# Two chained cross-attention layers: pairing the second layer's value sums, moving one set of transposes, and splitting a small softmax between VectorE and ScalarE

## The reference

```python
# layer 0: 8 heads of 40, 371 keys; the last 4 context rows are "tokens"
hs = mha(x @ Wq, enc @ Wk, enc @ Wv)
ca_q1 = einsum('btc,th->bch', ca, Wq_ca)[:, indices, :]    # 112 rows
ca_hs1 = mha(ca_q1, x, x)                                  # 112 x 112 softmax, 8 heads
ca_hs2 = mha(ca_hs1 @ Wq, ca @ Wk_ca, ca @ Wv_ca)          # 4 keys
x = (hs + ca_hs2) @ Wout + b_out + x
# layer 1: 20 heads of 16, 375 keys
x = mha(x @ Wq1, ctx @ Wk1, ctx @ Wv1) @ Wo + bo + x
```

## Time and profile before

| | |
|---|---|
| median of 3 runs | 744.45 us (744.38 to 744.81) |
| the profiled execution | 745.43 us |
| its span, first to last instruction | 743.6 us |
| mean granted TensorE clock | 0.981 |
| PE busy | 702.2 us, 94% |
| PE weight loads busy | 612.6 us, 82% |
| DVE busy | 470.8 us, 63% |
| ACT busy | 403.7 us, 54% |
| POOL busy | 294.8 us, 40% |

### The profile page before, as it was taken

One profiled execution on the slowest core, in us unless ns is written; L12 is line 12 of the kernel. 1 busy time (PEld: TensorE's weight loads), 2 busy tenths in 40 slices (PEclk: granted clock), 3 DMA queues, 4 the chain that ended last, 5 costly groups with the idle time before them and its releaser, 6 DMA issues.

```text
span 743.6 us, 18194 instructions
## 1 busy us (share of the span) xinstructions
PE 702.2 (94%) x6924; PEld 612.6 (82%) x6924; DVE 470.8 (63%) x1028; ACT 403.7 (54%) x923; POOL 294.8 (40%) x401
## 2 busy tenths in 40 slices
PE   8887999999999999999999999999999999999985
PEld 5576888888888888888888888888888888887763
DVE  2563666757576675757566675757667575757662
ACT  2554555555565555665555555556555555554422
POOL 5485662444334253443326245423525343321200
PEclk9889999999999999999999999999999999999986
DMA  9533453342616244252525334361524425160400
GB/s 326 171 106 91 119 130 81 101 88 76 138 47 142 65 120 97 67 118 59 136 58 137 82 92 93 77 136 47 142 69 115 103 65 122 21 143 19 80 9 9
DMA packets 52387, 72.45 MB, mean 97 GB/s; under 512 B 12128, under 2 KB 44256, under 8 KB 52304
## 3 DMA queue, kind: packets, MB, share of 16 engines
q1 hardware_dynamic: 44832, 60.34, 31.9%
q0 software_dynamic: 6144, 9.25, 6.5%
q10 hardware_dynamic: 1328, 1.71, 0.6%
HBM read 20.60 MB, written 4.26 MB: 33 GB/s over the span
## 4 chain that ended last, share of the span: by engine, by line
PE 73%; ACT 10%; DVE 9%; issue 3%; POOL 1%; ACTq 0%; POOLq 0%
PE bankX L1005 29%; PE bankO L1225 8%; PE bankST L1193 7%; PE bankS L1159 6%; PE bankST L1187 5%; ACT arena L577 4%; ACT arena L595 3%; DVE q1T L829 2%; DVE negmax L773 2%; PE bankX L1118 2%; PE bankX L1125 2%; PE bankX L1087 2%; PE bankS L1156 2%; PE bankX L1071 2%; ACT q1T L666 2%
## 5 line engine op out<-in xcount | busy, mean ns | idle before, releaser
L773 DVE TENSOR_REDUCE negmax<-bankS 112x2 f32<-112x750 f32 (+1 forms) x224 | 208.5, 931 | 57.3 <-PE bankS L1159 33.3
L494 POOL DMA_DIRECT2D k_stack<-stage x192 | 96.2, 509 | 180.3 <-DVE stage L809 153.1
L577 ACT ACTIVATE arena<-bankST 125x1344 f32<-125x1344 f32 x80 | 103.5, 1293 | 33.1 <-PE bankST L1193 33.1
L1225 PE MATMUL bankO<-arena,v 125*32 125x112 f32 (+2 forms) x2688 | 107.8, 265 | 6.1 <-ACT arena L577 4.6
L1225 PEld LDWEIGHTS bankO<-arena,v 125*32 125x32 f32 (+2 forms) x2688 | 81.6, 118 | 28.6 <-issue 13.6
L1159 PE MATMUL bankS<-k_stack,q1T 112*112 112x376 f32 x320 | 87.3, 354 | 3.6 <-DVE negmax L773 3.0
L1005 PE MATMUL bankX<-ctx_hi,WH 128*120 128x376 f32 (+2 forms) x192 | 69.0, 359 | 3.0 <-DVE qn L765 2.2
L457 POOL TENSOR_TENSOR w2bd<-w2s,cst 96x896 fp32r<-96x896 f32 x16 | 29.9, 1870 | 99.7 <-DVE w2s L765 99.7
L1193 PE MATMUL bankST<-q1T,k_stack 112*125 112x224 f32 x480 | 66.0, 274 | 0.0
L1005 PE MATMUL bankX<-WH,ctx_hi 128*125 128x320 f32 x192 | 66.0, 344 | 0.0
L1005 PE MATMUL bankX<-ctx_hi,WL 128*120 128x376 f32 (+2 forms) x192 | 64.1, 334 | 0.0
(11 more groups left out here) (141 smaller groups left out, 1546.1 us busy)
## 6 DMA issues: line engine op xcount, KB each, us to landing
k_stack<-stage SPq DMA_DIRECT2D x96, 176.2 KB
k_stack<-stage SPq DMA_DIRECT2D x192, 70.5 KB, 2.6
k_stack<-stage POOLq DMA_DIRECT2D x192, 47.0 KB, 2.0
ctx_raw<-in_ctxT SPq DMA_DIRECT2D x16, 376.0 KB, 3.4
k_stack<-stage SPq DMA_DIRECT2D x48, 117.5 KB
xp<-in_xpad SPq DMA_DIRECT2D x16, 224.0 KB, 3.4
x_raw<-in_xT SPq DMA_DIRECT2D x16, 168.0 KB, 2.4
out<-x1b SPq DMA_DIRECT2D x16, 140.0 KB, 3.3
```

Source lines behind the costliest of these rows:

```text
L494: pool.dma_start(dst, src).then_inc(k1_stacked_pool[b % 2], 16)
L577: nc.scalar.activation(dst[0:KC], bankST[0:KC, :, 0:GROUP * SQ], ACT.Exp).then_inc(exp_done, 1)
L773: nc.vector.tensor_reduce(negmax[:, n % 2, 2 * pair:2 * pair + 2], bankS[0:SQ, :, 0:keys], axis=AX, op=ALU.max, negate=True).then_inc(max_ ...
L1225: last = nc.tensor.matmul(dst, v, src[0:keys, c, SQ * j:SQ * j + SQ], start=(c == 0), stop=(c == NKC - 1))
```

## The change

1. **Pairs.** The groups of layer 1 are attended in episodes: groups 0 and 1 together, 2 and 3 together, 4 alone (`EPISODES`); layer 0 stays as it was. An episode is attended in the slot of its last group, so slots 5, 0 and 1, with nothing in slots 4 and 6. The pair's outputs lie side by side in `bankO` and are copied by one DVE instruction. `pv_done` and `o_copied` count episodes.
2. **Order of slot 1.** `N1a` goes ahead of `q0`, from phase 3 to phase 2.
3. **Token softmax.** After the maxima of S2_0 (S2_1), DVE adds them to the 448 scores and writes the result to `prob2`, which frees the bank. ACT takes one exponential of the 448 in place. `reciprocal2` first sums the 8 x 112 exponentials on DVE.

```diff
 UNITS = [
     ([("V1_0", -1)], [("q1T_0", -1)], [("V1_1", -1)], [("W2", 1), ("PV2", 0)]),
-    ([("q1T_1", -1), ("V1_2", -1)], [("q1T_2", -1)], [("q0", 1)], [("N1a", -2), ("K1_0", 0)]),
+    ([("q1T_1", -1), ("V1_2", -1)], [("q1T_2", -1)], [("N1a", -2), ("q0", 1)], [("K1_0", 0)]),
...
+EPISODES = [e for b in range(B + 1) for e in
+            ([[(0, b, 0)], [(0, b, 1)]] if b < B else []) +
+            ([[(1, b - 1, 0), (1, b - 1, 1)], [(1, b - 1, 2), (1, b - 1, 3)], [(1, b - 1, 4)]] if b > 0 else [])]
+EPISODE = {g: n for n, e in enumerate(EPISODES) for g in e}
+
+def attended_at(t, i):
+    late = scored_at(t, i, LAG)
+    return EPISODES[EPISODE[late]] if late and EPISODES[EPISODE[late]][-1] == late else None
...
             def exps2(b, half):
-                act.wait_ge(max2_done, 2 * b + half + 1)
-                X = bankX[bank(f"S2_{half}", b)]
-                for h in range(4 * half, 4 * half + 4):
-                    last = nc.scalar.activation(prob2[0:SQ, h, :], X[0:SQ, (h % 4) * SQ:(h % 4 + 1) * SQ], ACT.Exp,
-                                                bias=negmax2[:, h:h + 1], accum_out=sum2[:, h:h + 1])
-                last.then_inc(bank_drained[bank(f"S2_{half}", b)], 1)
+                act.wait_ge(bank_drained[bank(f"S2_{half}", b)], drained(f"S2_{half}", b))
+                scores2 = prob2[0:SQ, 4 * half:4 * half + 4, :].rearrange("p h k -> p (h k)")
+                nc.scalar.activation(scores2, scores2, ACT.Exp).then_inc(exp2_done, 1)
...
-            def copy_o(g):
+            def copy_o(groups):
...
-                    at = (2 + n % 2) * SQ
-                    dst, src = o1T[:, k, :], bankO[:, at:at + SQ]
+                    dst, src = o1T[:, k:k + len(groups), :], bankO[:, 2 * SQ:(2 + len(groups)) * SQ]
...
                                             op=ALU.max, negate=True).then_inc(max2_done, 1)
+                    dve.wait_ge(max2_done, 2 * b + i + 1)
+                    if b > 0:
+                        dve.wait_ge(unit_filled, filled(f"T2_{i}", b - 1))
+                    nc.vector.tensor_tensor(
+                        prob2[0:SQ, 4 * i:4 * i + 4, :], X[0:SQ, 0:4 * SQ].rearrange("p (h k) -> p h k", h=4),
+                        negmax2[:, 4 * i:4 * i + 4].unsqueeze(2).broadcast_to((SQ, 4, SQ)), ALU.add).then_inc(free, 1)
...
             def reciprocal2(b):
-                dve.wait_ge(bank_drained[bank("S2_0", b)], drained("S2_0", b))
-                dve.wait_ge(bank_drained[bank("S2_1", b)], drained("S2_1", b))
+                dve.wait_ge(exp2_done, 2 * b + 2)
+                nc.vector.reduce_sum(sum2[:, :], prob2[0:SQ], axis=AX).then_inc(sum2_done, 1)
+                dve.wait_ge(sum2_done, b + 1)
                 nc.vector.reciprocal(rsum2[:, :], sum2[:, :]).then_inc(rsum2_done, 1)
...
-            def attend(g, transposed):
-                layer, b, k = g
-                n = NUMBER[g]
-                pe.wait_ge(exp_done, n + 1)
+            def attend(groups, transposed):
+                n = EPISODE[groups[0]]
                 pe.wait_ge(mT_copied, transposed)
                 if n > 0:
                     pe.wait_ge(o_copied, n)
...
+                for g in groups:
+                    layer, b, k = g
+                    pe.wait_ge(exp_done, NUMBER[g] + 1)
...
```

More of the change, by code:

```diff
@@ L275, in xattn_kernel @@
         rsum2_done = sem("rsum2_done")
+        exp2_done = sem("exp2_done")
+        sum2_done = sem("sum2_done")
         prob2_ready = sem("prob2_ready")
@@ L568, in exps @@
                 if n >= 2:
-                    act.wait_ge(pv_done, n - 1)
+                    act.wait_ge(pv_done, EPISODE[GROUPS[n - 2]] + 1)
                 elif n == 1:
@@ L630, in unit @@
                     elif i == 0:
-                        act.wait_ge(pv_done, NUMBER[0, b - 1, 1] + 1)
+                        act.wait_ge(pv_done, EPISODE[0, b - 1, 1] + 1)
                     nc.scalar.activation(v0[0:KC, i, :].rearrange("p (h d) -> p h d", h=H0)[:, :, 0:D0],
@@ L638, in unit @@
                     elif i == 0:
-                        act.wait_ge(pv_done, NUMBER[1, b - 2, G1 - 1] + 1)
+                        act.wait_ge(pv_done, EPISODE[1, b - 2, G1 - 1] + 1)
                     nc.scalar.activation(v1[b % 2][0:KC, i, :].rearrange("p (h d) -> p h d", h=H1)[:, :, 0:D1],
@@ L779, in copy_mT @@
                 nc.vector.tensor_copy(mT[:, n % MT_BUFS, :], bank_mT).then_inc(mT_copied, 1)
-            def copy_o(g):
-                layer, b, k = g
-                n = NUMBER[g]
-                dve.wait_ge(pv_done, n + 1)
+            def copy_o(groups):
+                layer, b, k = groups[0]
+                dve.wait_ge(pv_done, EPISODE[groups[0]] + 1)
                 if layer == 0:
-                    dst, src = o0T[:, 2 * k:2 * k + 2, :].rearrange("p c q -> p (c q)"), bankO[:, 0:2 * SQ]
+                    dst, src = o0T[:, 2 * k:2 * k + 2, :], bankO[:, 0:2 * SQ]
                 else:
-                    at = (2 + n % 2) * SQ
-                    dst, src = o1T[:, k, :], bankO[:, at:at + SQ]
+                    dst, src = o1T[:, k:k + len(groups), :], bankO[:, 2 * SQ:(2 + len(groups)) * SQ]
+                dst = dst.rearrange("p c q -> p (c q)")
                 nc.vector.tensor_copy(dst, src).then_inc(o_copied, 1)
@@ L911, in _ @@
                 for i in range(SLOTS):
-                    g, before, late = scored_at(t, i), scored_at(t, i, 1), scored_at(t, i, LAG)
+                    g, before = scored_at(t, i), scored_at(t, i, 1)
                     if g:
@@ L928, in _ @@
                         unit(*u)
-                    if late:
-                        copy_o(late)
+                    if attended_at(t, i):
+                        copy_o(attended_at(t, i))
                     for u in units_of(t, i, 3):
@@ L1090, in unit @@
                     layer, k = {"N0": (0, 1), "N1a": (1, 3), "N1b": (1, 4)}[kind]
-                    pe.wait_ge(o_copied, NUMBER[layer, b, k] + 1)
+                    pe.wait_ge(o_copied, EPISODE[layer, b, k] + 1)
                     cols = [o0T[:, c, :] for c in range(4)] if layer == 0 else [
@@ L1205, in attend @@
                     pe.wait_ge(o_copied, n)
[L1206 to L1213, removed]
@@ L1214, in attend @@
-                for c, j in at_once:
-                    h = GROUP * k + j
+                for g in groups:
+                    layer, b, k = g
+                    pe.wait_ge(exp_done, NUMBER[g] + 1)
+                    if k == 0:
+                        for i in range(NKC):
+                            pe.wait_ge(bank_drained[bank(f"V{layer}_{i}", b)], drained(f"V{layer}_{i}", b))
+                    src = PT[:, NUMBER[g] % 2]
                     if layer == 0:
-                        keys = KC if c < 2 else KC - NTOK
-                        dst = bankO[64 * (j % 2):64 * (j % 2) + 64, (j // 2) * SQ:(j // 2 + 1) * SQ]
-                        v = v0[0:keys, c, 64 * h:64 * h + 64]
-                    else:
[L1221 to L1226, removed]
+                        at_once = [(c, j) for pair in range(2) for c in range(NKC) for j in (2 * pair, 2 * pair + 1)]
+                    else:
+                        at_once = [(c, j) for c in range(NKC) for j in range(GROUP)]
+                    for c, j in at_once:
+                        h = GROUP * k + j
+                        if layer == 0:
+                            keys = KC if c < 2 else KC - NTOK
+                            at = (j // 2) * SQ
+                            dst = bankO[64 * (j % 2):64 * (j % 2) + 64, at:at + SQ]
+                            v = v0[0:keys, c, 64 * h:64 * h + 64]
+                        else:
+                            keys = KC
+                            at = (2 + k % 2) * SQ
+                            dst = bankO[32 * j:32 * j + 32, at:at + SQ]
+                            v = v1[b % 2][0:keys, c, 32 * h:32 * h + 32]
+                        last = nc.tensor.matmul(dst, v, src[0:keys, c, SQ * j:SQ * j + SQ], start=(c == 0),
+                                                stop=(c == NKC - 1))
@@ L1263, in _ @@
                         unit(*u)
-                    if late:
-                        attend(late, transposed)
-                        attended = NUMBER[late] + 1
+                    if attended_at(t, i):
+                        attend(attended_at(t, i), transposed)
+                        attended = EPISODE[late] + 1
                     for u in units_of(t, i, 3):
```

## The result

The changed kernel took 764.98 us in the median of four runs (762.37 to 767.35), against 744.41 us for four runs of the kernel before (743.99 to 744.81): 1.0262 times as long, 95% interval 1.0224 to 1.0300. The forecast was 758 with a range of 743 to 768: the right way, and 7 us short.

The account below looks back on a forecast made before the run. PE was taken as the bound, busy 41.71 of 42.60 us an iteration. The terms 9.4 + 5.2 - 1.4 + 1.0 - 0.4 = 13.8 us on 744.45 gave 758.2, stated as 758, range 743 to 768.

Parts of the forecast that it names:

- slots 4 to 0: Late sum and pairs together make slot 1 begin 0.37 us late, 14 x 0.37 = 5.2 us.
- The order of slot 1: Slot 1: q0 stands about 1 us for q1T_2's drain; +0.72 us in 13 iterations, 9.4 us.
- The sum ahead of the drain: Slot 4: DVE's sum, 1.09 us, delays out1's drain, so N0 starts 0.64 us later; the next maxima and hn0T follow.
- Pairs: Slots 5 to 0: a pair takes about 1.23 us; q1's drain, uncovered in slot 6, makes V1_0 wait some 0.4 us.
- Slots 2 and 3: DVE's adds and ACT's one exponential bring slot 3's attend 0.1 us earlier, a gain of 1.4 us in all.
- Start: First element: POOL's normalisation waits for reciprocal2, now behind DVE's sum; +1.0 us.
- The covers hold: Rival: q0 and V1_0 don't stand, only gains are left, 1.4 us an iteration, 725 us in all; chance 0.17.
- DVE becomes the pace: Rival: DVE's added 2.3 us an iteration, ahead of maxima that scores wait for, isn't absorbed; 775 us; chance 0.07.

Follow-up runs that it names:

- e3: Kernel before with only the new order of slot 1 (N1a ahead of q0), no pairs, old token softmax; 758.85 us, ratio 1.0159.
- e5: Kernel before with the pairs alone, old order of slot 1 and old token softmax; 744.81 us, ratio 0.9966.
- e4: Kernel before with the changed token softmax alone, old order, no pairs; 753.80 us, ratio 1.0113.
- e8: Changed kernel with q0 one phase later, behind the attend of group 4; 760.63 us, ratio 1.0169 against the kernel before.
- e7: Kernel before with the changed token softmax but without DVE's sum, the reciprocal taken of the negated maxima; 746.80 us, ratio 1.0003.
- e6: Kernel before with one pair only, groups 1 and 2 of layer 1 attended together in slot 6; 742.85 us, ratio 0.9949.
- e9: Kernel before with one pair in slot 6 and six warm-up matmul calls in place of four; 745.53 us, ratio 1.0021 against the kernel before.

## Why the prediction was right, and where it was off

The three parts add up: order +0.84 (e3), pairs -0.27 (e5), softmax +0.58 (e4) give +1.15 us, and the changed kernel has +1.16. The forecast had +0.72, +0.37 for slots 4 to 0 and -0.10 for slots 2 and 3, +0.99.

- **The order of slot 1** was right in its mechanism: the wait, its releaser, and its length (0.95 us at `q0`, "about 1 us"). The term was too small, 0.72 for 0.84. `q0` started as forecast, 2.92 us after the shifted scores against 2.90, but takes 1.35 us to the attend in place of 1.26. Its first matmul is followed by the next after 0.24 us (mean of twelve); before the change it was 0.15. The idle isn't needed for that: `V1_2` in slot 1, directly behind transposes and without a wait, has 0.23 in the kernel before too, and e8's `q0`, with PE busy up to it, 0.24 (519.71 to 519.94 above; its weight load waited 0.17 us). But `V1_0`, behind scores and after a wait for its drain, has 0.25 in the changed kernel. `q0` now has both, transposes ahead of it and a wait, so which of them costs the 0.09 us is open.
- **The sum ahead of the drain** was priced at 1.09 us and took 1.06 (1065 ns in the mean of sixteen). The groups of instructions of the changed kernel (busy time in us, mean ns of one, idle time before them):

```profile
L893 DVE TENSOR_REDUCE sum<-arena 112x8 f32<-112x896 f32 x16 | 17.0, 1065 | 0.0
L854 DVE TENSOR_TENSOR arena<-bankX,negmax 112x448 f32<-112x448 f32 x32 | 20.0, 625 | 1.1
L609 ACT ACTIVATE arena<-arena 112x448 f32<-112x448 f32 x32 | 18.5, 577 | 46.5 <-DVE arena L854 46.5
```

  The line through the two maxima rows gave 1.09, and the estimate from the Trainium skill (VectorE: DVE Perf Modes, the errata table) 0.99; the measurement is between, nearer to the rows. Taking it out gave back 0.46 us (e7), less than the 0.66 by which `N0` is late, because `K0_2`'s wait of slot 4 then shows. The chain behind it went as written: `N0` (+0.66 for +0.64), the next maxima, `hn0T`.
- **Pairs.** 0.52 + 0.71 = 1.23 us was forecast for a pair and 1.28 measured, the uncovered drain of `q1` at `V1_0` as forecast. Slots 4 to 0 lost 0.39 for 0.37. The Trainium skill's rule (TensorEngine Tiling (Array Packing), Key Properties) that a change of tiling mode drains TensorE fits the break that a pair saves: 1.28 against twice 0.71 is 0.14 us for each pair, and e5 and e6 show the gain in the iteration. That the switch of mode makes the break was not tested by itself.
- **Slots 2 and 3.** "Gain 0.1 x 14" came out near its size, 0.07 us, in the changed kernel and in e7. What it left out is what the slots hand on: the late copy of the transposed maxima, ACT's DMA issue behind it, and with them `hn1T`'s drain, for which `K0_2` waits in slot 4. In the changed kernel that wait doesn't add to the sum's: DVE starts the sum 2.79 us after slot 4's first scores and started the reciprocal at 2.76 before. So the forecast's total is right here by luck as much as by reading; without the sum (e7) the same adds lose 0.12. The adds themselves took 625 ns for the 0.62 forecast, the exponential 577 for 0.54.
- **Start.** The sum's 1.0 us is there (the normalisation starts 5.06 us later, of which 4.1 were there before it). The granted clock at the start, some 3 us of the measured difference or more by the estimate above, wasn't in the forecast; the four runs of before had shown no spread (743.99 to 744.81).
- **The rivals.** "The covers hold" needed `q1T_2` drained before 462.1, and the drain did not move. "DVE becomes the pace" holds for slot 4 and, through `hn0T`, the start of slot 5 only.

The 7 us short: between the two profiled executions the difference is 21.9 us, 13.9 in twelve steady iterations and 8.0 outside them; the forecast had 11.9 and 1.9. The order's term makes most of the first 2 us. Of the 6 others, 4.1 are the late start before the first `w2bd` product, which comes with the clock and ahead of every changed instruction, and the 2 left lie in the first and last iterations, where no run took them apart. That the measured time lies near the upper end of the range is so in part the clock's doing.

## What to carry to other kernels

When units share buffers by turns, the order of the list is also a table of who waits for whom: before a unit is moved, look up which drain its neighbour inherits, and what long work had been running under that drain. Work that is batched to save breaks leaves the slots it came from, so batch it out of the slot in which nobody waits for a drain (e6), not wherever the pairs fall. And work shifted to a less busy engine costs time where that engine's list has a drain behind the new instruction: here one sum of 1.06 us cost 0.46 us of every iteration, and the engine that it relieved was off the path.

## What the runs showed of the hardware that was not expected

- The granted clock in the first 20 us takes one of two courses, though the instructions up to there are the same (kernel before and e3): the first `w2bd` product started at 19.66 us or at 23.91. The time doesn't keep all of it: e6 and e9, which differ in the warm-up alone, have it at 19.48 and 23.89 and spans of 740.2 and 743.2 us. Longer warm-up work didn't settle it (e9).
- At the full granted clock, a projection's first matmul on 320 columns is followed by the next after 0.15 us where it comes behind scores without a wait, and after 0.22 to 0.25 us behind transposes or an attend (`V1_2`, `out1`) or after a wait (`V1_0` in the changed kernel): some 0.1 us for each such start.
